# Packing the masks of a score unit and of a unit of maxima on four quadrants of TensorE in a windowed attention

## The chip, the core and the metric

The kernel runs on one core of one Trainium2 chip. Times are microseconds of the device, from the start to the end of one execution. The time of a kernel is the median of its runs.

## What is computed

Two blocks of a small hybrid network, one after the other, on an activation of 2 x 1024 tokens and 128 features. The change touches only the first layer, a sliding-window attention with 16 heads of 8 features and a window of 64:

```
scores = jnp.einsum('bhnqd,bhnkd->bhnqk', qb, k2) * scale
delta = qi - kj + win
valid = (delta >= 0) & (delta <= win)
bias = slopes[:, None, None] * delta.astype(jnp.float32)
scores = jnp.where(valid[None, None], scores + bias[None, :, None], -jnp.inf)
p = jax.nn.softmax(scores, axis=-1)
out = jnp.einsum('bhnqk,bhnkd->bhnqd', p, v2)
```

After it come a linear layer, two attentions with grouped keys, a location-weighted attention, a mixture of experts, an attention with relu, a feed-forward layer and another mixture of experts, with norms between.

## The kernel before

Each engine has an instruction stream of its own, written out by hand in program order, and semaphores set what waits for what. The first attention runs in eight passes (`PASSES`, index k), each one batch entry and one group of four heads (G = 4, KT = 8 token tiles of 128). Queries and keys of a pass lie in one of four stacks (`stacks[k % 4]`, in the tiles `stf`, `stf`, `rq`, `hz`), each float32 value as three bfloat16 parts: 72 rows, and 16 rows for the distance bias and the row maxima, 88 in all. A pass is done twice, in two forms:

- A **unit of maxima** (`max_unit(m)`, eight per pass) computes scores with queries on the partitions: 128 x 512 in PSUM bank 4 or 5. VectorE takes the maximum over keys (`tensor_reduce`, L1258, into `mxq`). When the eight units of a pass are reduced, TensorE transposes the maxima into bank 5 (`transposed_maxima`, L1724), VectorE splits them in three bfloat16 parts with five small operations (`step`, L1237 to L1245), and a DMA writes them as rows of the stack.
- A **score unit** (`score_unit(n)`, eight per pass, i = n % 8) computes the scores with keys on the partitions, with the maxima subtracted, in bank 0 or 1. ScalarE takes the exponential (L897, into `prob`), and `values` multiplies them with the values for half a pass (banks 2, 3, 6, 7).

Either unit begins with two **mask** matmuls (`masks`): an identity in bfloat16 times `band_a`, 0 inside the window and -1e30 outside, 512 columns each, one on PSUM partitions 0 to 63 and one on 64 to 127. Eight **product** matmuls of 88 rows x 64 columns and 128 moving columns add to it. `band_a` repeats itself after 64 rows, and a unit's first half uses its rows 0 to 63, its second half its rows 64 to 127, each picked by the identity from all 128.

The units of maxima run two passes ahead (`MAX_AHEAD` = 16). The loop over n = 0 to 63 issues score unit n, at i = 1 the transposition for pass k + 1 and the values of the last half pass, at i = 5 the values of the first half, and then one unit of maxima, m = 16 + n (in pass 0: two of them in each iteration from i = 4 on). From n = 48 on no units of maxima are left.

A score unit waits for the exponential of two units before (`q["ex"]`), a unit of maxima for the reduction of two units before (`w_m`). The unit u = 0 of a pass waits also for its stack's loads, and u = 1 for the first operation of the step for the pass before its own (`w_n`), since both use bank 5. After some units (m = 29, 33, 45, 49, 61) VectorE adds a copy that ScalarE makes of finished outputs (`add_half`, L1253; the copy is L889), which ScalarE makes after the exponential of n = 14, 18, 30, 34, 46.

In the profile a tile shape such as 128*64 is rows x columns of the stationary operand. `bsb` holds identity and band, so rows with `bsb` are masks; rows with 88*64 are products; `work,vbuf` are values. A float32 matmul is recorded as two instructions. All matmuls of the helper `mm` have line L1639.

Of the kernel before, what the change touches and what calls it, by code (L numbers as in the profile page):

```python
# [40 lines left out]
KT = S // P  # L41
# [6 lines left out]
HB = P // 2  # L48
# [54 lines left out]
def build(nc, xt, wp, vp, cp, bp, rope_q, rope_k, bias_q, bias_k, out):  # L103
    ctx = ExitStack()
    with ctx:
# [3 lines left out]
        def sem(name):  # L109
            return ctx.enter_context(nc.semaphore(name))  # L110
# [25 lines left out]
        for room in (stf[:, 0:G * (S + SL) // 2], stf[:, G * (S + SL) // 2:], rq[:], hz[:]):  # L136
            half = room.bitcast(BF16)
# [39 lines left out]
        def bank(i):  # L177
            return ps[:, i, :]

        def two(i):  # L180
            return ps[:, i:i + 2, :].rearrange("p a s -> p (a s)")
# [15 lines left out]
        def c_(name, rows=P):  # L197
            a, b = CAT[name]
            return csb[0:rows, a:b]

        def b_(name):
            a, b = BAT[name]
            return bsb[:, a:b]
# [4 lines left out]
        def ch(t, c):  # L208
# [83 lines left out]
            mm=sem("proj_in_psum"),  # L292
# [25 lines left out]
            u=sem("out_reciprocal_product"),  # L318
            rv=sem("out_reciprocal_done"),
            o=sem("out_normed"),  # L320
# [139 lines left out]
        PASSES = [(b, g) for b in range(B) for g in range(NG)]  # L460
# [47 lines left out]
        def stack_loads(k):  # L508
            return 16 * (8 + 7 * (k // 4))

        MAX_UNITS = KT
        MAX_AHEAD = 2 * KT
# [1124 lines left out]
        def _(pe):  # L1637
            def mm(o, l, r, start=True, stop=True):
                return nc.tensor.matmul(o, l, r, start=start, stop=stop, skip_group_check=True)  # L1639
# [31 lines left out]
            def weight_products():  # L1671
                pe.wait_ge(s_w1, 16)
                mm(ps[:, 0, 0:128], w_("f_re"), c_("dft_c"), True, False)
                mm(ps[:, 0, 0:128], w_("f_im"), c_("dft_s"), False, True).then_inc(s_fa, 1)
                mm(ps[:, 1, 0:128], w_("f_im"), c_("dft_c"), True, False)
                mm(ps[:, 1, 0:128], w_("f_re"), c_("dft_ns"), False, True).then_inc(s_fa, 1)
                pe.wait_ge(s_fb, 2)
                mm(ps[:, 2, 0:128], nsq[:, 0, 0:128], c_("idft_c"), True, False)
                mm(ps[:, 2, 0:128], nsq[:, 1, 0:128], c_("idft_ns"), False, True).then_inc(s_fa, 1)
                a0 = WAT["g_kup"][0]  # L1680
                mm(ps[:, 3, 0:96], w_("g_kvd", 32), wsb[0:32, a0:a0 + 96]).then_inc(s_fa, 1)
                for j in range(4):
                    for hd in range(G):
                        ins = mm(ps[32 * j:32 * j + 32, 6, hd * P:(hd + 1) * P], c_("dense")[:, 32 * hd:32 * hd + 32],
                                 w_("l_wo"))
                ins.then_inc(s_fa, 1)
                mm(ps[:, 7, 3 * P:3 * P + 2], c_("by_head"), vsb[:, VAT["r_bq"]:VAT["r_bq"] + 2])
                for k, name in enumerate(OUT_WEIGHTS):
                    ins = mm(ps[:, 7, k * P:(k + 1) * P], c_("dense"), w_(name))
                ins.then_inc(s_fa, 1)  # L1690

            def window_attention():
                rows = ROWS + XROWS
                pe.wait_ge(p_r1, 2 * NC)
                pe.wait_ge(q["vf"], NC)

                def masks(o):
                    for half in range(2):
                        mm(o[half * HB:(half + 1) * HB], b_("ident")[:, half * HB:(half + 1) * HB], b_("band_a"),
                           True, False)  # L1700

                def max_unit(m):

                    k, u = m // MAX_UNITS, m % MAX_UNITS
                    if u == 0:
                        pe.wait_ge(w_st[k % 4], stack_loads(k))
                    if u == 1 and k:
                        pe.wait_ge(w_n, 4 * (k - 1) + 1)
                    if m >= 2:
                        pe.wait_ge(w_m, m - 1)  # L1710
                    qs, ks = stacks[k % 4]
                    o, hd = bank(4 + m % 2), u // 2
                    masks(o)
                    for j in range(4):
                        t = 4 * (u % 2) + j
                        for half in range(2):
                            at = t * P + half * HB
                            ins = mm(o[half * HB:(half + 1) * HB, j * P:(j + 1) * P], qs[0:rows, hd, at:at + HB],
                                     ks[0:rows, hd, at:at + P], False, j == 3)
                    ins.then_inc(w_s, 1)  # L1720

                def transposed_maxima(k):
                    pe.wait_ge(w_m, MAX_UNITS * (k + 1))
                    nc.tensor.transpose(bank(5)[0:G * KT, 0:P], mxq[:, k % 2, :], c_("ident")).then_inc(w_t, 1)  # L1724

                def score_unit(n):

                    k, st, hd = n // KT, n % KT // G, n % G
                    if n % KT == 0:
                        pe.wait_ge(w_l[k % 2], 48 * (k // 2 + 1))  # L1730
                    if n >= 2:
                        pe.wait_ge(q["ex"], n - 1)
                    qs, ks = stacks[k % 4]
                    o = bank(n % 2)
                    masks(o)
                    for j in range(4):
                        for half in range(2):
                            at = (4 * st + j) * P + half * HB
                            w = min(P, S - at)
                            ins = mm(o[half * HB:(half + 1) * HB, j * P:j * P + w],  # L1740
                                     ks[0:rows, hd, PAD + at:PAD + at + HB], qs[0:rows, hd, at:at + w], False, j == 3)
                    ins.then_inc(q["sc"], 1)

                def values(k, st):
                    b, g = PASSES[k]
                    pe.wait_ge(q["ex"], KT * k + G * (st + 1))
                    if st == 0:
                        pe.wait_ge(q["vg"], k + 1)
                        if k and g % 2 == 0:

                            pe.wait_ge(q["oc"], k)
                    for j in range(4):
                        t = 4 * st + j
                        for half in range(2):
                            rows = slice(half * HB, (half + 1) * HB)
                            at = t * P + half * HB
                            end = min(at + P, S)
                            mid = min(end, (at // CH + 1) * CH)
                            for lo, hi in ((at, mid), (mid, end)):
                                if lo == hi:  # L1760
                                    continue
                                first = g % 2 == 0 and lo in (half * HB, CH)
                                for hd in range(G):
                                    ins = mm(two(6 - 4 * half)[32 * hd:32 * hd + 32, lo:hi], vr[rows, g % 2, t, hd],
                                             prob[rows, st, hd, j * P + lo - at:j * P + hi - at], first, False)
                    ins.then_inc(q["pv"], 1)

                for m in range(MAX_UNITS):
                    max_unit(m)
                transposed_maxima(0)  # L1770
                weight_products()
                for m in range(MAX_UNITS, MAX_AHEAD):
                    max_unit(m)
                pe.wait_ge(s_fb, 6)
                for n in range(KT * len(PASSES)):
                    k, i = n // KT, n % KT
                    score_unit(n)
                    if i == 1 and k + 1 < len(PASSES):
                        transposed_maxima(k + 1)
                    if i == 1 and k:  # L1780
                        values(k - 1, 1)
                    if i == 5:
                        values(k, 0)
                    if n < KT:
                        for m in range(MAX_AHEAD + 2 * i - KT, MAX_AHEAD + 2 * i - KT + 2):
                            if m >= MAX_AHEAD:
                                max_unit(m)
                    elif MAX_AHEAD + n < MAX_UNITS * len(PASSES):
                        max_unit(MAX_AHEAD + n)
                pe.wait_ge(q["ex"], KT * len(PASSES) - 1)  # L1790
                denominators(AW, 0)
                values(len(PASSES) - 1, 1)
# [338 lines left out]
            for v in range(B * KT + 2):  # L2131
# [7 lines left out]
                if v >= 2:  # L2139
                    u = v - 2  # L2140
# [230 lines left out]
```

## Time and profile before

| | before |
|---|---|
| median of 3 runs | 1024.35 us (1015.62, 1024.35, 1024.69) |
| profiled execution | 1023.21 us |
| its span, first to last instruction | 1021.1 us |
| TensorE busy | 948.7 us, 93% |
| ScalarE, VectorE, GpSimd busy | 540.0, 535.3, 147.7 us |
| mean granted clock | 0.948 |

The span is 2.1 us shorter than the execution's own time. The loop that is changed runs from 52 to 131 us of it. Matmuls overlap in the array, so a matmul's own duration is longer than the distance to the next one; distances between starts tell how long the array was taken.

### The profile page before, as it was taken

The numbers are of one execution on the slowest core, as the hardware profiler recorded it, in microseconds if no ns is written. First come the engines' busy times: TensorE is split into PE (matmuls) and PEld (weight loads), VectorE is DVE, ScalarE is ACT, GpSimd is POOL, SyncE is SP. The second block draws the span as 40 slices with busy tenths as digits, with TensorE's granted clock in tenths as the row PEclk, the third lists the DMA queues.
The fourth block names the chain that finished last, engine by engine and source line by source line (L and its number), as shares of the span: only waits on it lengthen the run. The fifth ranks groups of instructions, "written<-read, shape, count | busy, mean of one in ns | idle before, by whom it ended". The sixth has DMA issues, their size and how long they took to land.

```text
span 1021.1 us, 22819 instructions
## 1 busy us (share of the span) xinstructions
PE 948.7 (93%) x9990; PEld 436.0 (43%) x9990; DVE 535.3 (52%) x870; ACT 540.0 (53%) x767; POOL 147.7 (14%) x164
## 2 busy tenths in 40 slices
PE   7698978999999988988998999989999999999998
PEld 4476733433333335754443444434333333444443
DVE  4576545523324375665565525555666666423554
ACT  6044535889999856443765531256455454445121
POOL 3001120501001003120010120000223322004000
PEclk9899989899999997589998799999999999899999
DMA  7644050100000000000000057100000000001651
GB/s 205 215 128 125 7 218 0 42 2 2 2 2 2 2 1 1 3 3 2 0 1 0 1 135 138 62 1 1 2 2 2 2 2 2 0 1 43 160 123 52
DMA packets 16763, 43.16 MB, mean 42 GB/s; under 512 B 4844, under 2 KB 5292, under 8 KB 15244
## 3 DMA queue, kind: packets, MB, share of 16 engines
q1 hardware_dynamic: 15692, 39.51, 14.5%
q10 hardware_dynamic: 972, 2.20, 0.7%
q8 instruction: 79, 1.29, 0.5%
q14 instruction: 20, 0.16, 0.1%
HBM read 36.91 MB, written 4.55 MB: 41 GB/s over the span
## 4 chain that ended last, share of the span: by engine, by line
PE 82%; ACT 8%; DVE 6%; issue 2%; DMA 1%; POOL 1%; ACTq 0%; SPq 0%; DVEq 0%; POOLq 0%
PE ps L1639 82%; ACT nrr L816 1%; ACT nrr L818 1%; ACT nsq L809 1%; DVE mxq L1258 1%; ACT work L897 1%; POOL work L677 1%; ACT nrr L826 0%; ACT nrr L823 0%; DMA stf<-scr_k 0%; DVE aux L1451 0%; DVE work L1307 0%; DMA x<-in_x 0%; PE ps L2072 0%; DVE work L1363 0%
## 5 line engine op out<-in xcount | busy, mean ns | idle before, releaser
L1639 PE MATMUL ps<-rq,stf 32*64 32x512 f32 (+4 forms) x4096 | 208.4, 465 | 3.3 <-ACT hz L1001 1.6
L1639 PE MATMUL ps<-work,vbuf 64*32 64x128 f32 (+6 forms) x2992 | 195.5, 421 | 2.4 <-DVE nsq L1357 2.2
L1639 PE MATMUL ps<-hz,wsb 128*128 128x512 f32 (+1 forms) x352 | 161.9, 624 | 5.0 <-ACT nsq L842 2.5
L957 ACT ACTIVATE work<-ps 128x1024 f32<-128x1024 f32 x144 | 139.5, 1021 | 14.3 <-PE ps L1639 10.4
L1639 PEld LDWEIGHTS ps<-rq,stf 32*64 32x64 f32 x4096 | 97.5, 147 | 110.2 <-issue 84.1
L1019 ACT ACTIVATE work<-ps 128x1024 f32<-128x1024 f32 x72 | 73.6, 1024 | 75.7 <-PE ps L1639 75.7
L1639 PEld LDWEIGHTS ps<-work,vbuf 64*32 64x32 f32 (+1 forms) x2992 | 62.9, 111 | 116.1 <-issue 64.4
L1639 PEld LDWEIGHTS ps<-hz,wsb 128*128 128x128 f32 (+1 forms) x352 | 62.8, 192 | 85.3 <-issue 73.2
L1341 DVE TENSOR_TENSOR work<-work,csb 128x1024 f32<-128x1024 f32 (+1 forms) x40 | 40.7, 1018 | 97.2 <-ACT work L957 96.8
L1065 ACT ACTIVATE work<-ps 128x512 f32<-128x512 f32 x48 | 28.7, 597 | 117.2 <-PE ps L1639 117.2
L1639 PE MATMUL ps<-work,wsb 128*128 128x512 f32 (+1 forms) x176 | 87.0, 603 | 2.7 <-DVE work L1553 2.7
L1402 DVE TENSOR_SCALAR work<-ps 128x1024 f32<-128x1024 f32 (+3 forms) x72 | 68.5, 952 | 24.2 <-PE ps L1639 24.2
L897 ACT ACTIVATE work<-ps 128x512 f32<-128x512 f32 x64 | 37.4, 598 | 65.3 <-PE ps L1639 65.3
L1550 DVE TENSOR_TENSOR work<-ps,work 128x512 f32<-128x512 f32 x48 | 33.2, 691 | 64.0 <-ACT work L1065 40.8
L1639 PE MATMUL ps<-bsb 128*64 128x512 bf16 x256 | 53.1, 398 | 13.8 <-DMA stf<-scr_k 7.4
L1639 PE MATMUL ps<-nsq,csb 128*128 128x512 f32 (+3 forms) x152 | 53.3, 530 | 10.8 <-DVE nrr L1253 3.0
L809 ACT ACTIVATE nsq<-ps 128x512 f32<-128x512 f32 x40 | 23.5, 588 | 62.4 <-PE ps L1639 62.4
L1258 DVE TENSOR_REDUCE mxq<-ps 128x4 f32<-128x512 f32 x64 | 42.8, 688 | 22.3 <-PE ps L1639 21.3
L1639 PEld LDWEIGHTS ps<-work,wsb 128*128 128x128 f32 (+1 forms) x176 | 31.9, 189 | 50.0 <-issue 34.3
L738 POOL TENSOR_TENSOR work<-work,csb 128x512 f32<-128x512 f32 (+1 forms) x40 | 36.4, 911 | 106.7 <-ACT work L1019 106.7
L719 POOL TENSOR_SCALAR aux<-nsq,csb 128x1024 f32<-128x1024 f32 x8 | 24.2, 3025 | 156.8 <-DVE nsq L1328 110.4
L1639 PE MATMUL ps<-x,csb 128*128 128x512 f32 x64 | 35.6, 663 | 6.3 <-DMA x<-in_x 4.8
(200 smaller groups left out, 1172.9 us busy)
## 6 DMA issues: line engine op xcount, KB each, us to landing
stf<-scr_w SPq DMA_DIRECT2D x32, 256.0 KB, 4.5
stf<-scr_w SPq DMA_DIRECT2D x64, 128.0 KB, 3.3
stf<-scr_q SPq DMA_DIRECT2D x12, 192.0 KB
wsb<-in_w SPq DMA_DIRECT2D x1, 2192.0 KB, 12.5
rq<-in_rq SPq DMA_DIRECT2D x2, 1024.0 KB, 9.9
stf<-scr_k SPq DMA_DIRECT2D x9, 204.0 KB
rq<-scr_k SPq DMA_DIRECT2D x6, 204.0 KB
hz<-scr_k SPq DMA_DIRECT2D x6, 204.0 KB
```

Of the source, the lines that this page charges most:

```text
L719: nc.gpsimd.tensor_scalar(nums[:, b * S:(b + 1) * S], half_out[0][:, b * S:(b + 1) * S], c_("part")[:, 0:1], None, ALU.mult).then_inc(q["s ...
L738: nc.gpsimd.tensor_tensor(cells, cells, c_("keep").unsqueeze(1).unsqueeze(1) .broadcast_to(list(cells.shape)), ALU.mult).then_inc(q["mk"], 1)
L809: nc.scalar.activation(nsq[:, c], bank(c), ACT.Square).then_inc(n_sq, 1)
L897: nc.scalar.activation(prob[:, st, hd], bank(n % 2), ACT.Exp, scale=SCALE).then_inc(q["ex"], 1)
L957: nc.scalar.activation(probs_of(n)[:, 2 * k:2 * k + 2].rearrange("p h s -> p (h s)"), two(slot(2 * n + k)), ACT.Exp, scale=SCALE).then_inc ...
L1019: nc.scalar.activation(probs_of(n)[:, 0:2].rearrange("p h s -> p (h s)"), two(slot(2 * n)), ACT.Relu, scale=SCALE).then_inc(q["ex"], 1)
L1065: nc.scalar.activation(moe[:, 0, f % 2], bank(f % 2), ACT.Silu).then_inc(m_sg, 1)
L1258: nc.vector.tensor_reduce(mxq[:, k % 2, 4 * u:4 * u + 4], bank(4 + m % 2).rearrange("p (t s) -> p t s", t=4), AX.X, ALU.max).then_inc(w_m, 1)
L1341: nc.vector.tensor_tensor(cells, cells, c_("keep").unsqueeze(1).unsqueeze(1) .broadcast_to(list(cells.shape)), ALU.mult).then_inc(q["mk"], 1)
L1402: ins = nc.vector.tensor_scalar(to[:, :, lo:hi], src[:, :, lo:hi], SCALE, 0.0, ALU.mult, ALU.max)
L1550: nc.vector.tensor_tensor(product, bank(2 + f % 2), moe[:, 0, f % 2], ALU.mult).then_inc(m_su, 1)
L1639: return nc.tensor.matmul(o, l, r, start=start, stop=stop, skip_group_check=True)
```

## The change

Where a score unit has a unit of maxima in the same iteration (`beside`), the masks of both are issued together, ahead of the score unit's products (`masks_of_two`): four matmuls, each with 64 rows and 64 columns of the identity. The score unit's two masks use partitions 0 to 63 of identity and band, the unit of maxima's two use partitions 64 to 127. The waits of the unit of maxima (`max_ready`) move ahead of these masks. Its products follow the score unit's directly, ahead of transposition and values. The transposition for the next pass goes from i = 1 to i = 0. In pass 0 the first of an iteration's two units of maxima is paired and the second stays at the end with masks of its own. There are 44 such pairs, n = 4 to 47.

```diff
+                def masks_of_two(o, o2):
+                    for i, to in ((0, o), (1, o2)):
+                        rows = slice(i * HB, (i + 1) * HB)
+                        for half in range(2):
+                            mm(to[half * HB:(half + 1) * HB], b_("ident")[rows, rows], b_("band_a")[rows], True, False)
...
-                def max_unit(m):
+                def max_ready(m):
 
                     k, u = m // MAX_UNITS, m % MAX_UNITS
                     if u == 0:
...
                         pe.wait_ge(w_n, 4 * (k - 1) + 1)
                     if m >= 2:
                         pe.wait_ge(w_m, m - 1)
+
+                def max_unit(m, masked=False):
+
+                    k, u = m // MAX_UNITS, m % MAX_UNITS
                     qs, ks = stacks[k % 4]
                     o, hd = bank(4 + m % 2), u // 2
-                    masks(o)
+                    if not masked:
+                        max_ready(m)
+                        masks(o)
...
-                    masks(o)
+                    if beside is None:
+                        masks(o)
+                    else:
+                        max_ready(beside)
+                        masks_of_two(o, bank(4 + beside % 2))
...
-                    score_unit(n)
-                    if i == 1 and k + 1 < len(PASSES):
+                    beside = None
+                    if n < KT:
+                        beside = MAX_AHEAD + 2 * i - KT if 2 * i >= KT else None
+                    elif MAX_AHEAD + n < MAX_UNITS * len(PASSES):
+                        beside = MAX_AHEAD + n
+                    score_unit(n, beside)
+                    if beside is not None:
+                        max_unit(beside, True)
+                    if i == 0 and k + 1 < len(PASSES):
                         transposed_maxima(k + 1)
                     if i == 1 and k:
                         values(k - 1, 1)
                     if i == 5:
                         values(k, 0)
-                    if n < KT:
-                        for m in range(MAX_AHEAD + 2 * i - KT, MAX_AHEAD + 2 * i - KT + 2):
-                            if m >= MAX_AHEAD:
-                                max_unit(m)
-                    elif MAX_AHEAD + n < MAX_UNITS * len(PASSES):
-                        max_unit(MAX_AHEAD + n)
+                    if n < KT and beside is not None:
+                        max_unit(beside + 1)
```

TensorE's instructions before, at n = 8 (from its unit of maxima on) and n = 9: the wait for `max_taken` is `w_m`, for `max_step` is `w_n`, for `probs_by_scalar` is `q["ex"]`.

```order
138 L1639 MATMUL ps<-bsb 64x512 [waits max_taken,win_stack_loaded3]
139 L1639 MATMUL ps<-bsb 64x512
140 L1639 MATMUL ps<-hz 64x128 x8
141 L1639 MATMUL ps<-bsb 64x512 [waits probs_by_scalar]
142 L1639 MATMUL ps<-bsb 64x512
143 L1639 MATMUL ps<-stf 64x128 x8
144 L1724 MATMUL ps<-csb,mxq 32x128 [waits max_taken]
145 L1639 MATMUL ps<-work,vbuf 32x128 [waits probs_by_scalar]
146 L1639 MATMUL ps<-work,vbuf 32x128 x27
147 L1639 MATMUL ps<-work,vbuf 32x64 x4
148 L1639 MATMUL ps<-bsb 64x512 [waits max_taken,max_step]
149 L1639 MATMUL ps<-bsb 64x512
```

The same place now, the whole of n = 8 and n = 9.

```order
127 L1639 MATMUL ps<-bsb 64x512 [waits win_stack_loaded3,max_taken,probs_by_scalar,max_rows_loaded1]
128 L1639 MATMUL ps<-bsb 64x512 x3
129 L1639 MATMUL ps<-stf 64x128 x8
130 L1639 MATMUL ps<-hz 64x128 x8
131 L1736 MATMUL ps<-csb,mxq 32x128 [waits max_taken]
132 L1639 MATMUL ps<-bsb 64x512 [waits max_taken,max_step,probs_by_scalar]
133 L1639 MATMUL ps<-bsb 64x512 x3
134 L1639 MATMUL ps<-stf 64x128 x8
135 L1639 MATMUL ps<-hz 64x128 x8
136 L1639 MATMUL ps<-work,vbuf 32x128 [waits probs_by_scalar]
137 L1639 MATMUL ps<-work,vbuf 32x128 x27
138 L1639 MATMUL ps<-work,vbuf 32x64 x4
```

The transposition stands one iteration earlier; the values, which stood between it and the masks that wait for `max_step`, stand behind them; and the four masks carry the waits of both units.

## Rows read from the trace of the kernel before

**Rows 1.** The page: busy time, and the granted clock in 40 slices.

```profile
PE 948.7 (93%) x9990; PEld 436.0 (43%) x9990; DVE 535.3 (52%) x870; ACT 540.0 (53%) x767; POOL 147.7 (14%) x164
...
PEclk9899989899999997589998799999999999899999
```

**Rows 2.** Waits of TensorE, 54 to 131 us: total, times, longest.

```profile
PE ps L1639 <- DVE mxq L1258: 3.0, 4, 0.8
PE ps L1639 <- ACT work L897: 1.4, 5, 0.3
PE ps L1639 <- issue: 1.0, 1, 1.0
PE ps L1724 <- DVE mxq L1258: 0.7, 1, 0.7
```

**Rows 3.** Timeline, undisturbed iterations: start, duration, what [idle before].

```profile
85.75 0.41 PE L1639 MATMUL ps<-bsb 128*64 128x512 bf16 x2
...
85.99 0.39 PE L1639 MATMUL ps<-stf 88*64 88x128 bf16 x8
...
86.22 0.38 PE L1639 MATMUL ps<-bsb 128*64 128x512 bf16 x2
...
86.43 0.69 DVE L1258 TENSOR_REDUCE mxq<-ps 128x4 f32<-128x512 f32 x1 [0.18 <-PE ps L1639]
86.44 0.39 PE L1639 MATMUL ps<-hz 88*64 88x128 bf16 x8
...
86.87 0.60 ACT L897 ACTIVATE work<-ps 128x512 f32<-128x512 f32 x1 [1.64 <-PE ps L1639]
```

**Rows 4.** Timeline, around transposition and values.

```profile
84.15 0.44 PE L1639 MATMUL ps<-hz 88*64 88x128 bf16 x8
...
84.52 0.29 PE L1724 MATMUL ps<-csb,mxq 128*32 128x128 f32 x1
...
84.73 1.09 PE L1639 MATMUL ps<-work,vbuf 64*32 64x128 f32 x64
...
84.84 0.28 DVE L1237 TENSOR_SCALAR aux<-ps 32x128 f32<-32x128 f32 x1
...
90.55 0.41 PE L1639 MATMUL ps<-bsb 128*64 128x512 bf16 x2
...
90.79 0.39 PE L1639 MATMUL ps<-stf 88*64 88x128 bf16 x8
...
101.96 0.39 PE L1639 MATMUL ps<-stf 88*64 88x128 bf16 x8
...
102.28 1.20 PE L1639 MATMUL ps<-work,vbuf 64*32 64x128 f32 x72
```

**Rows 5.** Timeline, float32 matmuls of 512 columns in a later layer.

```profile
885.06 3.60 PE L1639 MATMUL ps<-work,wsb 128*128 128x512 f32 x8
888.49 3.60 PE L1639 MATMUL ps<-hz,wsb 128*128 128x512 f32 x8
```

**Rows 6.** Timeline, iteration n = 16.

```profile
70.86 0.59 ACT L889 ACTIVATE nsq<-ps 128x512 f32<-128x512 f32 x1
...
71.49 0.62 DVE L1253 TENSOR_TENSOR nsq<-ps,nsq 128x448 f32<-128x448 f32 x1 [0.87 <-ACT nsq L889]
71.51 0.41 PE L1639 MATMUL ps<-bsb 128*64 128x512 bf16 x2
...
72.03 1.28 DVE L1258 TENSOR_REDUCE mxq<-ps 128x4 f32<-128x512 f32 x2
...
72.86 0.41 PE L1639 MATMUL ps<-bsb 128*64 128x512 bf16 x2 [0.71 <-DVE mxq L1258]
```

**Rows 7.** Timeline, the transposition for the last pass.

```profile
117.21 0.28 PE L1724 MATMUL ps<-csb,mxq 128*32 128x128 f32 x1 [0.73 <-DVE mxq L1258]
```

**Rows 8.** Timeline, the hole, and the loop's last masks.

```profile
91.02 0.38 PE L1639 MATMUL ps<-bsb 128*64 128x512 bf16 x1
92.36 0.38 PE L1639 MATMUL ps<-bsb 128*64 128x512 bf16 x1 [0.96 <-issue]
...
129.82 0.41 PE L1639 MATMUL ps<-bsb 128*64 128x512 bf16 x2
```

More of the change, by code:

```diff
@@ L1724, in transposed_maxima, with score_unit @@
                     nc.tensor.transpose(bank(5)[0:G * KT, 0:P], mxq[:, k % 2, :], c_("ident")).then_inc(w_t, 1)
-                def score_unit(n):
+                def score_unit(n, beside=None):
                     k, st, hd = n // KT, n % KT // G, n % G
```

## The prediction, made before the changed kernel ran

> **What bounds the kernel now.** I read the page first: TensorE is busy 93% of the span, and its clock stands at its upper level in slices 3 to 5, the first attention's loop [rows 1]. Then the waits of TensorE from 54 to 131 us, that loop: 3.0 us for VectorE's maxima, 1.4 us for ScalarE, one 1.0 us "issue" and 0.7 us of the transposition [rows 2]. So TensorE sets the pace here, with a few waits left. The timeline gives the rhythm [rows 3]: masks 85.75, products 85.99, masks 86.22, products 86.44. A unit is 0.22 us of masks and 0.22 us of products, an iteration (one unit of scores, one of maxima) 0.88 to 0.89. VectorE's reduction starts 0.44 us after its unit's products (85.99 to 86.43) and shows 0.69; ScalarE's exponential starts 0.43 after its own (86.44 to 86.87) and shows 0.60. Two reductions in a row show 1.28 [rows 6], so they follow at 0.60.
>
> **What the packing saves.** 44 iterations (n = 4 to 47) have a unit of maxima to pair. Two mask matmuls of 512 columns on two column groups take 0.22 us; four on four quadrants, if all run at once, take the same, and 44 x 0.22 = 9.7 us go. That row groups run at once is seen in the values: 64 float32 matmuls of 128 columns on 64 x 32 tiles take 1.02 us (84.73 to 85.75) with a change of tile shape behind them, 0.9 without it, or 0.11 for each eight [rows 3, 4]. Eight float32 matmuls of 512 columns take 3.43, 0.43 each [rows 5], so one of 128 takes 0.11: eight tiles in both row halves ran together. The bound on the other side is no overlap of row groups, 0.44 for the four and nothing saved. I take 0.22: the values are the nearest row, with the same two row halves in different banks.
>
> **What the new tile shape costs.** From masks to products the shape stays today (128 or 88 rows, 64 columns). Where it changes, time is lost [rows 4]: products at 101.96 are followed by values at 102.28, 0.32 later and not 0.22 (0.37 at 84.15, before the transposition), and masks behind values take 0.24 to their products (90.55 to 90.79), not 0.22. That is 0.10 ahead of a change and 0.02 behind it, 0.12, with 0.17 as the upper end. A change of rows alone stands there too: the transposition on 128 x 32 starts at 84.52 and the values on 64 x 32 at 84.73, 0.21 later, where 128 float32 columns stream in 0.11: 0.10 again. The new masks are on 64 x 64, the products stay on 88 x 64, so every iteration gets two changes. A pass has 5 today (in and out of transposition and values at i = 1, of values at i = 5). Then it has 19: 8 from the quads to products, 5 straight from products to the next quads, 6 in and out of transposition and two values, which now stand apart. Extra are 14 in each of five passes, 8 in the first and 1 at n = 48: 79 x 0.12 = 9.5 us. A new iteration is 0.24 + 0.10 + 0.24 + 0.22 + 0.10 = 0.90 against 0.885: the saving is eaten. These rows are all of changes to or from 32 columns; with none where the columns stay at 64, free changes would leave -9.7 here and not -0.2.
>
> The Trainium skill, page "TensorEngine Tiling (Array Packing)", section Key Properties, makes no such difference: changing the tiling mode, not merely the tile, drains the engine. By that rule the -0.2 holds; it speaks against the change, and the trace agrees with it by the 0.10.
>
> **What the moved transposition costs.** The transposition for pass k + 1 goes from i = 1 to i = 0, for the unit of maxima u = 1, paired at i = 1, waits for the first of VectorE's five step operations, which reads bank 5 before that unit overwrites it. Today the values, 1.02 us, stand between the two and nobody waits [rows 4]. Then nothing does. From the start of the products of u = 0: 0.44 to the reduction, 0.60 until VectorE is free, 0.28 for the step's first operation (84.84, [rows 4]), some 0.06 to TensorE, 1.38. TensorE is ready after 0.32 of products and 0.21 of transposition, 0.53. It waits 0.85 at n = 9, 17, 25, 33 and 41: 4.2 us. Queued behind the waiting masks are the score unit and the values, so ScalarE gets its scores as late.
>
> **What the earlier wait for maxima costs.** Today a wait for a reduction stands behind the score unit, which fills 0.45 of it. At n = 16, 20, 32 and 36 VectorE is late: it waits for ScalarE's copy of finished outputs (70.86), adds it (71.49), and only then reduces (72.03). TensorE's masks of maxima come at 72.86, the score unit n = 16 had run from 71.51 [rows 6]. Now that unit waits too and is still to be done: 4 x 0.45 = 1.8 us. The transposition for the last pass waits 0.73 at 117.21 behind two score units [rows 7]; moved, it has one ahead and one behind, 0.45, and the one at n = 0 the same. Together 2.7. In pass 0 an iteration has two units of maxima, the first paired. The next quad waits for the first one's reduction: 0.44 + 0.69 + 0.06 = 1.19 from its products, with 0.22 + 0.44 + 0.10 of work in between and no score unit. That is up to 0.43 three times, 1.3; between that and 0, since TensorE has short waits there already, I take 0.9.
>
> No transfer comes later for it: no wait on a DMA is left in this stretch [rows 2], and loads are triggered by the scores of a pass, so they move with the loop. No other engine gets an instruction more or less.
>
> **Sum.** -9.7 + 9.5 + 4.2 + 2.7 + 0.9 = +7.6 us. The loop's end is on the path, and the 16 last score units only shift. The profiled execution took 1023.2 us (span 1021.1 and 2.1 around it) and would take 1030.8; the median of the three runs is 1.1 above it, 1024.35, so the forecast is **1032 us**.
>
> **The rivals.**
> (a) A change of row groups alone is free. The 9.5 goes, but the 9.7 is not all gained: two iterations can't be shorter than 0.22 + 0.22 + 0.44 + 0.69 + 0.06 = 1.63, masks to masks over VectorE's reduction, 0.82 each. That gives 0.07 in some 28 iterations and 0.22 in the 12 beside values and 4 of pass 0's, some 5: 7.6 - 9.5 + 9.7 - 5 = +2.8, 1027 us. The row-only change at 84.52 speaks against it.
> (b) Not slower: (a), and the 0.85 behind the transposition is won back at the next late reduction, because that hangs on ScalarE's copy and not on TensorE: 2.8 - 4.2 = -1.4, 1023 us. It decides if ScalarE's copy stays where it is in time. Against it: the copy follows the exponential of n = 14, which is fed by the same late TensorE. The page's Theoretical Speedup (the Trainium skill) names up to 2x for a contraction of 64 or less, which by itself would give 1024.35 - 9.7 = 1014.7; the 1.63 bars that.
> (c) Slower by more: row groups don't run at once for these masks. The 9.7 stays, a little of it inside waits, so some 8.5: 1040.5 us. It decides from 0.3 us for four masks on. The values speak against it.
> (d) A change costs 0.16, as before the transposition at 84.15: 79 x 0.04 = +3.2, 1035 us.
> The 1.3 us hole from 91.02 to 92.36, of which 0.96 is called "issue" [rows 8], may go, double or move in any case. That the change doesn't do what it says is ruled out by the order of the instructions.
>
> **How the numbers follow.** The three runs lie 9 us apart, so about 1% is what a measurement of this kernel can tell from no change. Chances: forecast 0.58, (a) 0.14, (b) 0.05, (c) 0.08, (d) 0.15. Slower by over 1% is above 1034.6: all of (c), two thirds of (d), 0.09 of the forecast, 0.27. Faster by over 1%, below 1014.1, would take a run of the low kind, 0.03. The rest, 0.70, is within 1%, where the forecast itself stands with +0.75%. The range leaves out (c) and most of (b), and holds (a) and (d) with the hole: 1024 to 1037.
>
> **What the changed profile would show.** Quads whose products start 0.32 to 0.34 behind them show packing and change right; 0.22 would be (a), over 0.5 (c). Products of maxima to the next quad: 0.32. At n = 9, 17, 25, 33, 41 a wait of some 0.85 for VectorE's step right behind the transposition. At n = 16, 20, 32, 36 a wait for maxima with no score unit in it. The loop's last masks, 129.82 before [rows 8], at about 137. I am wrong if the masks' wait for two engines at once costs more than the later of the two, or if the holes let the clock fall.

## The result, and the profile after

The changed kernel takes 1039.24 us (median of four runs, 1035.91 to 1044.12), against 1023.97 us before on the same chip: a ratio of 1.0187, 95% interval 1.0144 to 1.023. It is slower by some 15 us, and lies above the range that was forecast. Its profiled execution took 1035.91 us, span 1033.8, 12.7 more than before.

The page of the changed kernel, busy time and granted clock, answers to [rows 1]. The loop, 51 to 148 us, lies in digits 3 to 6 of the clock's line.

```profile
PE 949.6 (92%) x9990; PEld 430.9 (42%) x9990; DVE 535.7 (52%) x870; ACT 540.5 (52%) x767; POOL 147.8 (14%) x164
...
PEclk9898699999999999589999699999999999899999
```

TensorE's busy time is the same to 1 us. Digits 4 and 5, 9 and 9 before, are 8 and 6 now. The changed kernel's stretches from 52 us to the end of its loop, with TensorE's granted clock behind the five engines:

```profile
52.00:64.00 12.00, 9.97 (x244) 6.76 (x244) 7.17 (x15) 5.26 (x9) 0.00 (x0) 1.00 0.37 100
64.00:76.00 12.00, 9.80 (x297) 6.81 (x297) 7.13 (x15) 5.16 (x9) 0.65 (x2) 1.00 0.41 122
76.00:91.00 15.00, 12.97 (x280) 9.02 (x280) 6.10 (x13) 4.18 (x8) 0.65 (x2) 0.66 0.24 70
91.00:105.00 14.00, 10.09 (x297) 6.76 (x294) 7.03 (x14) 5.54 (x10) 3.48 (x3) 0.97 0.36 95
105.00:121.00 16.00, 14.35 (x265) 9.47 (x267) 6.63 (x14) 4.07 (x7) 0.65 (x2) 0.50 0.29 81
121.00:133.00 12.00, 10.93 (x320) 7.48 (x318) 7.80 (x14) 5.79 (x10) 0.65 (x2) 1.00 0.02 5
```

0.50 is the lower of the clock's two levels, 1.2 GHz. A mean of 0.66 over 15 us is some 10 us at it; with the 0.97 and the 16 us at 0.50, TensorE ran at it for 27 us of the loop. Before, the mean from 52 to 131 us was 1.00.

The waits of TensorE from 52 to 145 us, to be read beside [rows 2]:

```profile
PE ps L1639 <- DVE mxq L1258: 6.1, 7, 1.5
PE ps L1639 <- ACT work L897: 4.4, 8, 0.8
PE ps L1639 <- issue: 3.0, 4, 1.2
PE ps L1736 <- DVE mxq L1258: 1.3, 2, 1.0
```

The waits for maxima doubled and the longest is 1.5. The 4.4 us put down to ScalarE are mostly not ScalarE's, as the timeline of n = 8 and 9 shows:

```profile
62.89 0.41 PE L1639 MATMUL ps<-stf 88*64 88x128 bf16 x8
...
63.14 0.39 PE L1639 MATMUL ps<-hz 88*64 88x128 bf16 x8
63.35 0.60 ACT L897 ACTIVATE work<-ps 128x512 f32<-128x512 f32 x1 [1.26 <-PE ps L1639]
...
63.46 0.28 PE L1736 MATMUL ps<-csb,mxq 128*32 128x128 f32 x1
63.57 0.69 DVE L1258 TENSOR_REDUCE mxq<-ps 128x4 f32<-128x512 f32 x1 [0.57 <-PE ps L1639]
64.18 0.27 DVE L1237 TENSOR_SCALAR aux<-ps 32x128 f32<-32x128 f32 x1
...
64.55 0.41 PE L1639 MATMUL ps<-bsb 64*64 64x512 bf16 x4 [0.81 <-ACT work L897]
...
64.89 0.25 PEld L1639 LDWEIGHTS ps<-stf 88*64 88x64 bf16 x8 [0.23 <-issue]
64.89 0.41 PE L1639 MATMUL ps<-stf 88*64 88x128 bf16 x8
...
65.14 0.39 PE L1639 MATMUL ps<-hz 88*64 88x128 bf16 x8
```

The exponential ended at 63.95, but the masks came at 64.55, 0.10 after VectorE's first step operation (64.18 to 64.45). A wait for several semaphores is put down to one of them; the one whose end fits is VectorE's. The four masks are one group, products follow 0.34 behind them, and the transposition's masks stand 1.09 behind it where 0.21 was free: 0.88 of waiting.

The timeline of the changed kernel at n = 16 and 17, to be read beside [rows 6], and what follows:

```profile
72.57 0.59 ACT L889 ACTIVATE nsq<-ps 128x512 f32<-128x512 f32 x1
...
72.75 0.41 PE L1639 MATMUL ps<-hz 88*64 88x128 bf16 x8
...
73.19 0.62 DVE L1253 TENSOR_TENSOR nsq<-ps,nsq 128x448 f32<-128x448 f32 x1 [2.24 <-ACT nsq L889]
73.73 1.28 DVE L1258 TENSOR_REDUCE mxq<-ps 128x4 f32<-128x512 f32 x2
...
74.56 0.41 PE L1639 MATMUL ps<-bsb 64*64 64x512 bf16 x4 [1.40 <-DVE mxq L1258]
...
75.47 0.28 PE L1736 MATMUL ps<-csb,mxq 128*32 128x128 f32 x1
...
76.56 0.51 PE L1639 MATMUL ps<-bsb 64*64 64x512 bf16 x4 [0.81 <-ACT work L897]
...
78.00 1.93 PE L1639 MATMUL ps<-work,vbuf 64*32 64x128 f32 x64
...
79.86 0.54 PE L1639 MATMUL ps<-bsb 64*64 64x512 bf16 x4
```

TensorE idles 1.40 at n = 16 with the score unit behind the wait, then 0.88 (1.09 less the 0.21 that was free) at n = 17, and from 76.7 on everything lasts twice as long: the values take 1.86 to the next masks, and not 1.02.

At n = 33 the same wait behind the transposition is put down to "issue", though the masks start 0.10 after VectorE's first step operation again:

```profile
107.64 0.27 DVE L1237 TENSOR_SCALAR aux<-ps 32x128 f32<-32x128 f32 x1
...
108.01 0.64 PE L1639 MATMUL ps<-bsb 64*64 64x512 bf16 x4 [0.69 <-issue]
```

So 0.7 of the 3.0 us of "issue" is this wait, and 2.3 are holes that no wait explains.

The changed kernel's last masks, which answer to 129.82 in [rows 8]:

```profile
148.16 0.41 PE L1639 MATMUL ps<-bsb 128*64 128x512 bf16 x2
```

### The profile page after: what moved, and what is told of

Same layout as the page of the kernel before. It is cut to its first block, busy times and chain, and to the rows that moved or that the text cites. A ratio compares the mean times of both kernels' runs of the same rounds, so it can differ in the third digit from the quotient of the medians.

```text
span 1033.8 us, 22852 instructions
## 1 busy us (share of the span) xinstructions
PE 949.6 (92%) x9990; PEld 430.9 (42%) x9990; DVE 535.7 (52%) x870; ACT 540.5 (52%) x767; POOL 147.8 (14%) x164
## 4 chain that ended last, share of the span: by engine, by line
PE 81%; ACT 8%; DVE 6%; issue 2%; DMA 1%; POOL 1%; ACTq 0%; SPq 0%; DVEq 0%; POOLq 0%
PE ps L1639 81%; ACT nrr L816 1%; ACT nrr L818 1%; DVE mxq L1258 1%; ACT nsq L809 1%; ACT work L897 1%; POOL work L677 1%; DVE work L1363 1%; ACT nrr L826 0%; ACT nrr L823 0%; DMA stf<-scr_k 0%; DVE aux L1451 0%; DVE work L1307 0%; ACT work L986 0%; PE ps L2091 0%
## 5 line engine op out<-in xcount | busy, mean ns | idle before, releaser
L1639 PE MATMUL ps<-rq,stf 32*64 32x512 f32 (+4 forms) x4096 | 203.8, 453 | 4.8 <-DVE stf L1316 1.6
L1639 PEld LDWEIGHTS ps<-rq,stf 32*64 32x64 f32 x4096 | 93.7, 141 | 111.1 <-issue 80.5
L1639 PE MATMUL ps<-bsb 64*64 64x512 bf16 (+1 forms) x256 | 37.8, 445 | 19.7 <-DMA stf<-scr_k 7.1
```

## The experiments

One number is read from each profiled execution below: the loop's length, from the masks of n = 0 to the last masks. It is 77.75 before (52.07 to 129.82) and 96.83 changed (51.33 to 148.16). Two theories were set against each other. Theory 1, the order: the new waits leave TensorE idle, and the clock falls for it. Theory 2, the packing: four quadrants at once let the clock fall. All kernels below were compared with the kernel before on their own chip, where it took 1019.3 to 1020.6 us.

**The order alone.** The masks are unpacked, the order and the waits stay.

```diff
-                        masks_of_two(o, bank(4 + beside % 2))
+                        masks(o)
+                        masks(bank(4 + beside % 2))
```

> The changed kernel's order and waits, but the masks of the two units are four matmuls of 128 rows, two by two, as before: no change of tile shape between masks and products, nothing packed. Read at the loop's last masks (129.8 us before, 148.2 changed). Theory 1, the order: the waits cost 7.6 us and their idle time lets the clock fall, which costs the rest; then this kernel too ends the loop at 137 or later, with stretches of granted clock 0.5, and takes 1030 to 1040 us. Theory 2, the packing: four quadrants at once are what lets the clock fall; then the clock stays at 1.0 here and the loop ends at 137 to 138.

1031.44 us, ratio 1.0132 (1.0086 to 1.0177). The loop took 91.57, 13.8 more than before, with one stretch of 6.8 us at the lower clock, behind n = 16 and 17 (77.5 to 84.4), and 1.9 us of "issue". So without any packed masks most of the loss is there and the clock falls. That speaks for theory 1, though the stretch is shorter than in the changed kernel. The same two waits came again at n = 32 and 33, and there the clock stayed up, 1.00 from 104 to 121 us:

```profile
105.23 0.62 PE L1639 MATMUL ps<-bsb 128*64 128x512 bf16 x4 [1.42 <-DVE mxq L1258]
...
107.31 0.62 PE L1639 MATMUL ps<-bsb 128*64 128x512 bf16 x4 [0.80 <-ACT work L897]
```

**Packing without the new waits.** The masks of the unit of maxima are packed with those of the score unit that follows.

```diff
-                        max_unit(MAX_AHEAD + n)
+                        max_unit(MAX_AHEAD + n, n + 1 if pairs(n) else None)
...
-                    masks(o)
...
+                        score_ready(ahead)
+                        masks_of_two(o, bank(ahead % 2))
```

> The order of before, but the masks of the unit of maxima of iteration n are packed with those of score unit n + 1, which follows it anyway (40 pairs). Transposition and values stay where they were, so the waits of the changed kernel don't arise; packing and changes of shape do. Theory 1: clock at 1.0, loop's last masks at 129 to 131, time as before within 2 us: the pairs save 8.8 and their changes of shape cost 8.6. Theory 2: the clock falls here too, last masks at 137 or later. If changes of row groups were free: 125 to 126.

1018.83 us, ratio 1.001 (0.9987 to 1.0032), last masks at 130.21, loop 77.49, clock at its upper level throughout the loop. 40 pairs are packed, and the time doesn't change: saving and changes of shape about cancel, and packed masks don't lower the clock. Its timeline of one undisturbed stretch:

```profile
86.86 0.41 PE L1639 MATMUL ps<-bsb 64*64 64x512 bf16 x4
87.20 0.41 PE L1639 MATMUL ps<-stf 88*64 88x128 bf16 x8
87.45 0.39 PE L1639 MATMUL ps<-hz 88*64 88x128 bf16 x8
87.77 0.41 PE L1639 MATMUL ps<-bsb 64*64 64x512 bf16 x4
```

0.34 + 0.25 + 0.32 = 0.91 an iteration, where it was 0.885. Of its loop 3.3 us are "issue" (1.0 before), one hole of 2.10 among them, behind which the clock stayed up. Without such holes it would be an estimated 2.6 shorter than before, not 0.3. Its other waits are 3.8 us where they were 5.1, which is half of that; what the rest is was not tried.

**Shape alone.** Before, with masks of 64 rows in the units of maxima from n = 8 on, nothing packed or moved.

```diff
+                def masks_64(o):
+                    for half in range(2):
+                        mm(o[half * HB:(half + 1) * HB], b_("ident")[0:HB, 0:HB], b_("band_a")[0:HB], True, False)
...
-                    masks(o)
+                    (masks_64 if m >= MAX_AHEAD + KT else masks)(o)
```

> Before, with nothing packed or moved: only the two masks of each unit of maxima from n = 8 on use 64 rows of identity and band in place of 128 (40 units, 70 changes of shape more). If a change costs 0.12 us, last masks at 137 to 138 less what falls into waits that are there anyway (1 to 2 us), so 136 to 138, and products start 0.32 to 0.34 behind such masks. If a change of rows alone is free: 129.8 and 0.22 to 0.24. Both theories expect the clock at 1.0.

1025.74 us, ratio 1.0049 (1.0022 to 1.0077), loop 81.64, clock at the upper level. Its timeline:

```profile
88.62 0.39 PE L1639 MATMUL ps<-hz 88*64 88x128 bf16 x8
88.94 0.40 PE L1639 MATMUL ps<-bsb 64*64 64x512 bf16 x2
89.28 0.41 PE L1639 MATMUL ps<-stf 88*64 88x128 bf16 x8
89.53 0.39 PE L1639 MATMUL ps<-bsb 128*64 128x512 bf16 x2
89.75 0.39 PE L1639 MATMUL ps<-hz 88*64 88x128 bf16 x8
```

The columns stay 64 wide, only the rows change, and it costs 0.32 into and 0.34 out of the masks in place of 0.22 twice: the iteration is 1.13 (88.62 to 89.75), 0.24 more. That is 0.12 a change, and rival (a) falls. The end came earlier than expected (133.60, not 136 to 138). 70 changes at 0.12 are 8.4 us, and the loop is 3.9 longer: its execution had no "issue" hole (1.0 before), and the waits for maxima fell from 3.0 to 1.1 us, that of the transposition from 0.7 to 0.4. The 1.3 us that are left are not explained.

**The waits filled.** The changed kernel with extra mask matmuls ahead of the waits. They write to the score unit's bank, whose real masks overwrite them.

```diff
+                        for _ in range(5 if n in (16, 20, 32, 36) else 3 if n >= KT and n % KT == 1 else 0):
+                            masks(o)
                         max_ready(beside)
                         masks_of_two(o, bank(4 + beside % 2))
```

> The changed kernel with filler matmuls where it waits: before the packed masks at n = 16, 20, 32, 36 five extra pairs of masks, and at n = 9, 17, 25, 33, 41 three, written to the score unit's own bank and overwritten by its real masks. They run in time in which TensorE waits anyway. Theory 1: the clock stays at 1.0 through the loop, last masks at 137 to 138, time 1029 to 1032, 7 or more below the changed kernel. Theory 2: the clock falls all the same, 145 or later.

1027.08 us, ratio 1.0071 (1.004 to 1.0102): 7.4 us over the kernel before, with 70 matmuls of 512 columns more than the changed kernel. It is below the 1029 to 1032 expected, since the kernel before took less on this chip than in the first measurement (1019.68 against 1023.97). The loop took 85.09, 7.34 more than before, last masks 137.39, and the clock stayed at its upper level. The timeline at n = 16 and 17:

```profile
73.90 1.26 PE L1639 MATMUL ps<-bsb 128*64 128x512 bf16 x10
75.49 0.41 PE L1639 MATMUL ps<-bsb 64*64 64x512 bf16 x4 [0.32 <-DVE mxq L1258]
75.83 0.41 PE L1639 MATMUL ps<-rq 88*64 88x128 bf16 x8
76.08 0.39 PE L1639 MATMUL ps<-stf 88*64 88x128 bf16 x8
76.40 0.28 PE L1736 MATMUL ps<-csb,mxq 128*32 128x128 f32 x1
76.61 1.24 PE L1639 MATMUL ps<-bsb 128*64 128x512 bf16 x10
77.78 0.41 PE L1639 MATMUL ps<-rq 88*64 88x128 bf16 x8
78.03 0.39 PE L1639 MATMUL ps<-stf 88*64 88x128 bf16 x8
78.35 1.09 PE L1639 MATMUL ps<-work,vbuf 64*32 64x128 f32 x64
```

The waits are as long as in the changed kernel (products at 73.67 to masks at 75.49 is 1.82, the transposition at 76.40 to products at 77.78 is 1.38, where it was 63.46 to 64.89), but TensorE works in them, and the values behind take 1.02 again. This is the forecast's kernel, so to say: its order, its shapes, its waits, without the clock. Two cautions. This execution had no "issue" hole either, so it doesn't part the waits from the holes by itself. And it took 1023.44 us, near the lowest of the kernel's ten (1022.97 to 1033.08); whether the clock stayed up in the loop of the other nine no trace shows.

**One of the two waits taken away.** In the first, the transposition is back at i = 1 and u = 1 unpaired; in the second, n = 16, 20, 32 and 36 are unpaired, with the score unit ahead of the wait.

```diff
-                    elif MAX_AHEAD + n < MAX_UNITS * len(PASSES):
+                    elif i != 1 and MAX_AHEAD + n < MAX_UNITS * len(PASSES):
...
-                    if i == 0 and k + 1 < len(PASSES):
+                    if i == 1 and k + 1 < len(PASSES):
...
+                    if n >= KT and i == 1 and MAX_AHEAD + n < MAX_UNITS * len(PASSES):
+                        max_unit(MAX_AHEAD + n)
```

> The changed kernel with the transposition back at i = 1 and the unit of maxima u = 1 not paired (its own masks, behind the values); 39 pairs are left, and the waits at n = 16, 20, 32, 36. Undone are the five waits of 0.85 behind the transposition (4.2 us) and the 0.9 of the transpositions at n = 0 and 48; lost is nothing, since a pair is worth about 0. Loop's last masks at 132 to 133 with the clock at 1.0. If the wait behind the transposition is what lets the clock fall, it stays up here; if the waits at n = 16, 20, 32, 36 do it, there are cold stretches here and the loop ends at 135 or later.

1027.77 us, ratio 1.0086 (1.0056 to 1.0117); loop 86.49, 10.2 us at the lower clock, 2.7 of "issue". The last masks came at 137.90, where 132 to 133 was expected with the clock up and 135 or later with it down.

```diff
-                    score_unit(n, beside)
+                    alone = n in (16, 20, 32, 36)
+                    score_unit(n, None if alone else beside)
                     if beside is not None:
-                        max_unit(beside, True)
+                        max_unit(beside, not alone)
```

> The changed kernel with n = 16, 20, 32, 36 not paired: there the score unit goes first with its own masks and the unit of maxima waits alone behind it, as before. 40 pairs and the waits of 0.85 behind the transposition are left. Undone are 4 x 0.45 = 1.8 us. Loop's last masks at 135.5 to 136.5 with the clock at 1.0. If the waits at n = 16, 20, 32, 36 are what lets the clock fall, it stays up here; if the wait behind the transposition does it, there are cold stretches and the loop ends at 139 or later.

1031.11 us, ratio 1.0122 (1.0087 to 1.0157); loop 89.67, 6.8 us at the lower clock, 4.2 of "issue"; last masks at 141.33, as expected if the clock falls (139 or later). 1.6 of the 4.2 are again the waits behind the transposition, at n = 17 and 33 (0.80 each), so the holes are 2.6.

The clock fell in both kernels, but not each time behind the wait that was left. With the late maxima alone it fell for 3.4 us behind the wait of 1.40 at n = 16 (from 73.8), and for 6.8 us (from 97.7) behind an "issue" hole:

```profile
96.85 0.32 PE L1639 MATMUL ps<-work,vbuf 64*32 64x64 f32 x8 [1.99 <-issue]
```

With n = 16, 20, 32 and 36 unpaired it fell from 76.7, behind a wait for maxima that is still 0.96 long and the 0.80 behind the transposition, and from 127.9, behind the last pass's transposition (1.00). So this pair doesn't isolate the second kind of wait; the next does. Taking half of the cold time and the holes over 1.0 off the lengths leaves 79.7 and 84.7, 1.9 and 6.9 over the kernel before; the forecast's terms were 7.6 - 4.2 - 0.9 = 2.5 and 7.6 - 1.8 = 5.8.

**One of the two waits filled, beside the changed kernel.** The filler of above with one of its two conditions.

> The changed kernel once more, beside the next two on one chip. Cold stretches in the loop again, though not of the same length; 1030 to 1042 us, ratio to before 1.012 to 1.020, last masks at 143 to 150.

> The changed kernel with filler matmuls only ahead of the packed masks at n = 16, 20, 32, 36 (five extra pairs each). If those waits are what lets the clock fall, last masks at 137 to 138 as with all waits filled; if the wait behind the transposition does it too, a cold stretch or two stay and the loop ends at 139 to 143.

> The changed kernel with filler matmuls only ahead of the packed masks at n = 9, 17, 25, 33, 41 (three extra pairs each). If the waits at n = 16, 20, 32, 36 let the clock fall, the cold stretches stay and the loop ends at 141 or later; if it is the wait behind the transposition, 137 to 138. I expect the former to be the stronger, since those waits are the longer ones (1.5 against 0.88).

| | median us | ratio to before (95%) | loop | at lower clock | "issue" |
|---|---|---|---|---|---|
| changed again | 1033.37 | 1.0127 (1.0079 to 1.0175) | 94.51 | 20.5 | 2.4 |
| n = 16, 20, 32, 36 filled | 1030.78 | 1.0094 (1.0058 to 1.013) | 89.60 | 3.4 | 1.7 |
| behind the transposition filled | 1030.43 | 1.0111 (1.0068 to 1.0154) | 91.63 | 10.2 | 2.0 |

The changed kernel again has cold stretches, five of them: the first two behind the same waits as in its first profile (n = 17 and n = 20), the others elsewhere. Of its 2.4 of "issue" 0.7 is the wait behind the transposition at n = 33. With the waits for maxima filled one stretch is left. It begins at 67.9, behind these two, and the four later waits of 0.81 let nothing fall:

```profile
65.51 0.41 PE L1639 MATMUL ps<-bsb 64*64 64x512 bf16 x4 [0.37 <-DVE mxq L1258]
...
67.50 0.41 PE L1639 MATMUL ps<-bsb 64*64 64x512 bf16 x4 [0.81 <-ACT work L897]
```

With the other kind filled three are left, from 84.8, 101.9 and 112.1, each behind a wait for maxima of 1.40 to 1.47 (n = 20, 32, 36); the one at n = 16, 1.40 too, let nothing fall. So either kind of wait can be followed by a fall without the other, and neither is each time. Filling the longer ones shortens the cold time more, as expected, in one profiled execution each; with both filled it was gone. In time the two half-filled kernels can't be told from the changed one: their intervals overlap. The first came out longer than I expected: last masks at 143.87, not 139 to 143. Its loop began 2 us late (54.27), and its 89.60 with 3.4 cold is some 2 us more than the terms give; 0.6 of that is a wait at 103.47 for the load of a stack's rows, which neither profile of the changed kernel has. The rest I can't explain.

**Pairs only behind values.** The kernel with the other pairing, but with the 10 pairs whose masks follow values.

```diff
                 def pairs(n):
-                    return True
+                    return n % KT in (1, 5)
```

> The order of before with masks packed only where a change of shape is paid anyway: the unit of maxima that follows values (n with i = 1 or 5) is paired with the next score unit, 10 pairs. Such a pair saves 0.22 and adds one change, 0.10 to 0.12, for the values are left by a change in any case: 10 x 0.11 = 1.1 us less, last masks at 128.5 to 129, clock at 1.0, and a ratio to before of 0.997 to 1.001 that a timing can hardly tell from 1.

1018.15 us against 1019.26, ratio 0.9989 (0.9967 to 1.0011); loop 76.92, 0.8 shorter than before, though its last masks came at 130.26, not at 128.5 to 129, since its loop began late (53.34). The sign is as expected, but a timing can't tell it from no change. No version was found that beats the kernel before beyond doubt.

## Why the prediction was wrong

- **What the packing saves: right.** The four masks start together and their products come at 0.34, so row groups ran at once; (c) was wrong, though its 1040.5 us lay next to the result.
- **What the new shape costs: right.** 0.12 a change, forecast from changes to and from 32 columns, was measured with the columns fixed ("shape alone"). With 40 pairs and no new waits the time stayed within 0.3% of before. Rivals (a) and (b) fall, and of (d) nothing is seen.
- **The transposition: right.** 0.88 of waiting behind it, forecast 0.85.
- **The earlier wait for maxima: right in kind, too small in size.** It holds the score unit back, and the idle time at n = 16 grew by 0.69 (0.71 to 1.40), not by 0.45. The four waits are 1.40, 1.47, 1.40 and 1.46 in the kernel with the other kind filled, 5.7 together, where they were 2.9: 2.8 more, forecast 1.8.
- **The sum of these: right, a little low.** +7.6 was forecast. With the clock kept up by filler the loop is 7.34 longer, or 8.3 if the hole of 1.0 is counted out, which the kernel before had in its loop and the filled one had not. That the medians differ by 7.4 too is no second proof, for the clock in the loop is known of one execution only. The small terms (0.9 for pass 0, 0.45 each for the transpositions at n = 0 and 48) were not tried one by one.
- **What failed is the step from the sum to the time.** Its working took each wait at its own length, with every row of the loop at the upper clock, and named a falling clock only as its last sentence, with no price and no chance. What the runs showed in its place: the new idle time, 0.88 in five passes and some 1.4 at n = 16, 20, 32 and 36, let the clock fall. "Issue" holes have a part in it that no run separates: the 17.1 us began at 104.1, in the wait at n = 32, with holes of 0.89 and 1.17 ahead of it. TensorE ran at half speed for 27 us of the loop in one profiled execution, for 20.5 in another. Half of that, 10 to 14 us, is the most it can cost; where TensorE waits in such a stretch it costs less. In the loop: 19.1 more, of which 8.3 by the sum, 1.3 by holes (2.3 against 1.0), and the 9.5 left by the clock. In the times, the filler takes the ratio from 1.0187 and 1.0127 to 1.0071; the interval of the first stands clear of the filled kernel's (1.0144 against 1.0102), that of the second overlaps it.
- The profiled execution grew by 12.7 us only, since its loop began 0.7 earlier and what lies behind the loop was 5.6 shorter than in the profile of before. By the mean granted clock (0.948 and 0.945) the lower level held for 106 us of the span before and for 114 changed, 27 of these in the loop, so outside the loop for some 19 us less. The change doesn't touch those layers; I take this for the difference between two executions: what lies behind the loop is the same code in all twelve kernels and took 882.7 to 891.3 us in their profiles, 884.9 in the changed kernel's second.

Why "issue" holes grew from 1.0 to some 2 or 3 us in most of the variants, and were absent in two, was not tried and stays open.

## What to carry to other kernels

A wait on the busiest engine costs its length, and then what it may do to the clock: before a reorder puts a wait ahead of independent work, ask what the engine does in it, and give the clock a price and a chance of its own. Packing small matmuls pays only if the tile shape stays: one change in and one out ate 0.22 us of saving here. And if two waits are joined at one instruction, everything that stood between them is exposed.

## What the hardware showed that was not expected

- TensorE's clock fell to 1.2 GHz with the engine idle for 1.40 and 0.88 us within 4 us (73.2 to 76.6), and busy otherwise; before, with 0.71 us at that place, it had not. The Trainium skill, page "TensorE: Matmul & The Clock Gate", section Why this matters for your kernels, warns of long idle gaps between bursts of matmuls; here it fell behind two short ones, and the trace decides.
- Such gaps don't let it fall each time: behind 1.42 and 0.80 us (the order alone, n = 32 and 33) and behind a single hole of 2.10 us (packing without the new waits) it stayed up. What decides between them no run here shows.
- The stretches at the lower clock lasted 3.4, 6.8 and 17.1 us, and differed from execution to execution of one kernel.
- Work that computes nothing made a kernel faster: with 70 filler matmuls it took 1027.08 us, 1.0071 times the kernel before on its chip (1019.68), and without them 1033.37, 1.0127 times it (1020.55), in another set of runs. These two intervals overlap (1.004 to 1.0102, 1.0079 to 1.0175); the changed kernel's first (1.0144 to 1.023) stands clear.
